# Messages of layer L2 in a four-network graph kernel: half of the tiles' source products built on TensorE and VectorE, the other half gathered

## The reference, cut to what matters

```python
h_src = h[src]
W_rel = jnp.matmul(w_comp, V).reshape(num_rels, in_dim, out_dim)   # 90 x 16 x 16
e = jnp.concatenate([h_src @ Ws.T, he @ Ws.T, h[dst] @ Ws.T], axis=1) @ Wa.T
msg = jnp.einsum('ei,eio->eo', h_src, W_rel[rel_type]) * e
h_out = jax.ops.segment_sum(msg, dst, num_segments=n_nodes)
```

## Time and profile before

| | us |
|---|---|
| median of 3 runs | 8560.5 (8557.9 to 8567.8) |
| the profiled execution, its own time | 8550.3 |
| its span in the profile | 8548.6 |
| the `y_tab` block, in the trace | 5984.4 to 6116.8 |
| `message_pass`, in the trace | 6116.8 to 7202.1 |

### The profile page before, as it was taken

One profiled execution on the slowest core, in us unless ns is written; L12 is line 12 of the kernel. 1 busy time (PEld: TensorE's weight loads), 2 busy tenths in 40 slices (PEclk: granted clock), 3 DMA queues, 4 the chain that ended last, 5 costly groups with the idle time before them and its releaser, 6 DMA issues. The chain is left out here.

```text
span 8548.6 us, 233535 instructions
## 1 busy us (share of the span) xinstructions
PE 6428.4 (75%) x55142; PEld 5292.3 (62%) x55143; DVE 4918.4 (58%) x13561; ACT 2820.3 (33%) x8471; POOL 5192.9 (61%) x7408
## 2 busy tenths in 40 slices
PE   1222215767699998999899989997866666888998
PEld 1111113555477776888688868886455555887998
DVE  7333345867455655666466646664322223998999
ACT  1222212545333333333333333332133333222554
POOL 2777754756477766777577757774277775222554
PEclk8555556555599999999999999998555555999999
DMA  2000003434388886888688878885200001332232
GB/s 66 3 3 3 3 29 104 120 97 120 88 221 216 216 197 181 222 221 222 161 222 222 222 164 223 222 222 121 95 7 7 7 7 24 82 82 57 73 73 59
DMA packets 1319112, 1000.54 MB, mean 117 GB/s; under 512 B 479354, under 2 KB 1223183, under 8 KB 1318092
## 3 DMA queue, kind: packets, MB, share of 16 engines
q1 hardware_dynamic: 941322, 649.30, 27.7%
q0 software_dynamic: 134272, 178.98, 10.8%
q10 hardware_dynamic: 243392, 170.76, 6.9%
HBM read 951.88 MB, written 54.19 MB: 118 GB/s over the span
## 5 line engine op out<-in xcount | busy, mean ns | idle before, releaser
L1480 POOL DMA_INDIRECT qg<-q_tab,qidx x2520 | 2389.2, 948 | 940.1 <-issue 699.2
L1635 DVE COPY ps<-b 128x384 f32<-128x384 f32 x1120 | 628.0, 561 | 1381.2 <-ACT h L1600 1374.8
L1067 PE MATMUL ps<-rhs_i,ohi 128*128 128x128 f32 (+2 forms) x8640 | 1215.7, 266 | 210.1 <-issue 197.2
L1067 PEld LDWEIGHTS ps<-rhs_i,ohi 128*128 128x128 f32 (+1 forms) x8640 | 1000.4, 163 | 342.5 <-issue 282.0
L1033 POOL COPY near<-x 128x48 bf16 x2160 | 675.9, 351 | 789.4 <-PE ps L1056 434.0
L1195 POOL DMA_INDIRECT got_m<-y_tab,idx_m x832 | 815.8, 981 | 478.8 <-issue 251.4
L1549 PE MATMUL ps<-ohm,h 128*128 128x128 f32 x6720 | 1032.9, 290 | 65.3 <-DVE ps L1635 33.9
L1549 PEld LDWEIGHTS ps<-ohm,h 128*128 128x128 f32 x6720 | 838.8, 192 | 257.7 <-issue 242.8
L1593 ACT ACTIVATE h<-ps,b 128x384 f32<-128x384 f32 x1120 | 650.2, 581 | 1052.2 <-PE ps L1531 955.6
L375 POOL DMA_INDIRECT list_by_src<-ring,rpos x808 | 783.1, 969 | 349.0 <-issue 255.0
L1212 PE MATMUL ps<-rhs_m,ohi_m 128*128 x2880 | 668.1, 403 | 416.1 <-ACT rhs_m L1238 387.3
(11 more groups left out here) (442 smaller groups left out, 8623.6 us busy)
## 6 DMA issues: line engine op xcount, KB each, us to landing
pb<-p_tab ACTq DMA_DIRECT2D x1680, 96.0 KB
pb<-p_tab SPq DMA_DIRECT2D x1680, 96.0 KB
places<-place_by_turn SPq DMA_DIRECT2D x560, 192.0 KB
places_i<-place_by_meeting SPq DMA_DIRECT2D x360, 256.0 KB, 3.4
places_i<-place_by_meeting SPq DMA_DIRECT2D x720, 128.0 KB, 3.1
qb<-q_tab SPq DMA_DIRECT2D x840, 64.0 KB
qg<-q_tab,qidx POOLq DMA_INDIRECT x2520
nears<-near_by_turn SPq DMA_DIRECT2D x560, 64.0 KB
```

Of the source, the lines that this page charges most:

```text
L1067: m = pe.matmul(ps[:, bass.ds(to[j], width)], ohi[:, h, j, :], rhs[:, h, j, 0:width], start=False, stop=True, skip_group_check=True)
L1480: pool.indirect_dma_start(qg[:, h, j, :], None, q_tab, IndirectOffsetOnAxis(ap=qidx[:, h, j:j + 1], axis=0)).then_inc(m_got[h], 16)
```

## The change

It splits each group of 4 tiles into the first two and the last two. The last two are gathered from `y_tab` as before. For the first two, the edge's source row (17 numbers: 16 features and the gate's part) comes from a product of a one-hot matrix `ohx` (node place against edge) with the source block's rows `xq`, and the edge's relation matrix (256 numbers) from a product of a one-hot `ohr` (relation against edge) with the 90 matrices in three bf16 parts, `w_parts`. VectorE multiplies the two and sums over the 16 inputs. The sums at the destinations stay as they are, but their place in TensorE's order is now fixed: group N-16 (`LAG` = 16) right behind the products of group N, and the last 168 groups after all products. VectorE's `build` is placed 12 groups behind (`AHEAD = LAG - U`).

More of the change, by code:

```diff
@@ L592, in gnn_kernel @@
             loc_s = sb("loc_s", [P, NT], F32, st)
+            rel_f = sb("rel_f", [P, NT], F32, st)
+            at_x = sb("at_x", [1, NT], I32, st)
+            rel_rows = sb("rel_rows", [P, 8, P], BF16, st)
             blk_s = sb("blk_s", [1, NT], F32, st)
@@ L716, in _ @@
                     v_chain(dve, dve.tensor_scalar(blk_s[0:1, :], blkt[0:1, :], float(P), None, ALU.mult))
+                    v_chain(dve, dve.tensor_scalar(at_x[0:1, :], blkt[0:1, :], 17.0, float((NB - 1) * 17), ALU.mult, ALU.min))
                     dve.wait_ge(b_l, 16)
@@ L836, in _ @@
                     m.then_inc(c_w, 1)
+                    for c in range(8):
+                        m = pe.transpose(banks[6 + c // 4][0:C8, (c % 4) * P:(c % 4 + 1) * P], rel_f[:, c * C8:(c + 1) * C8], ident[:, :])
+                    m.then_inc(c_rel, 1)
                     pe.wait_ge(c_const, 2)
@@ L1164, in summed, with message_pass @@
             return ps[:, 512 * k:512 * k + 56 * n].rearrange("p (b c) -> p b c", c=56)
-        d_idx, d_rhs, d_ohi, d_sum, d_part, d_at = (sem("d_" + n) for n in ("idx", "rhs", "ohi", "sum", "part", "at"))
+        d_idx, d_rhs, d_ohi, d_sum, d_part, d_at, d_oh, d_w, d_xs, d_prod, d_m, d_gate = (
+            sem("d_" + n) for n in ("idx", "rhs", "ohi", "sum", "part", "at", "oh", "w", "xs", "prod", "m", "gate"))
         d_got = [sem(f"d_got{h}") for h in range(U)]
-        def message_pass():
+        d_pl = [sem(f"d_pl{h}") for h in range(U)]
+        LAG = 4 * U
+        assert (LAG - 2) * G >= NT2 - -(-E // P) + NB - 1 and NGI % U == 0 and K > 5
+        def message_pass(xq, w_parts):
             with ExitStack() as st:
-                idx = sb("idx_m", [P, U, G], I32, st)
-                got = sb("got_m", [P, U, G, 17], F32, st)
+                idx = sb("idx_m", [P, U, 2], I32, st)
+                got = sb("got_m", [P, U, 2, 17], F32, st)
                 ohi = sb("ohi_m", [P, U, G, P], F32, st)
@@ L1178, in message_pass, with x_bank @@
                 at_m = sb("at_m", [1, NIN * 2], I32, st)
+                at_x = sb("at_xm", [1, NT], I32, st)
+                pl = sb("pl_m", [P, U, 2 * P], BF16, st)
+                rl = sb("rl_m", [NREL, U, 2 * P], BF16, st)
+                ohx = sb("ohx_m", [P, U, 2 * P], F32, st)
+                ohr = sb("ohr_m", [NREL, U, 2 * P], BF16, st)
+                xs = sb("xs_m", [P, U, 2, 17], F32, st)
+                prod = sb("prod_m", [P, 2, 512], F32, st)
+                def x_bank(h):
+                    return banks[2 + h % 2][:, 0:34].rearrange("p (j f) -> p j f", j=2)
                 with nc.Block() as block:
@@ L1214, in sums @@
                             m.then_inc(d_sum, 1)
-                        turns(pe, sums, KI)
+                        def both(k, h):
+                            products(k, h)
+                            if not isinstance(k, int) or k >= LAG // U:
+                                sums(k * U + h - LAG, h)
+                        for k in range(5):
+                            for h in range(U):
+                                both(k, h)
+                        with pe.Fori(5, K) as k:
+                            for h in range(U):
+                                both(k, h)
+                        with pe.Fori(0, (NGI - NG + LAG) // U) as k:
+                            for h in range(U):
+                                sums(k * U + h + NG - LAG, h)
                     @block.scalar
@@ L1236, in step @@
[L1236 to L1240, removed]
+                            rows(k, h)
+                            if there(k, h, 1):
+                                messages(*moved(k, h, -1))
@@ L1253, in build, with step @@
                                               dst_i[:, bass.ds(n * G, G)][:, :, None].to_broadcast([P, G, P]), ALU.is_equal).then_inc(d_ohi, 1)
-                        turns(dve, build, KI)
+                        AHEAD = LAG - U
+                        def step(k, h):
+                            onehots(k, h)
+                            if there(k, h, 1):
+                                multiply(*moved(k, h, -1))
+                            if not isinstance(k, int) or k * U + h >= AHEAD:
+                                build(k * U + h - AHEAD, h, not isinstance(k, int) or k * U + h >= LAG)
+                            if there(k, h, 1):
+                                add_up(*moved(k, h, -1))
+                        for k in range(5):
+                            for h in range(U):
+                                step(k, h)
+                        with dve.Fori(5, K) as k:
+                            for h in range(U):
+                                step(k, h)
+                        multiply(K - 1, U - 1)
+                        add_up(K - 1, U - 1)
+                        with dve.Fori(0, (NGI - NG + AHEAD) // U) as k:
+                            for h in range(U):
+                                build(k * U + h + NG - AHEAD, h)
         def turn_block(src, f, dst, extra=None):
@@ L1935, in _ @@
                     def _(dve):
+                        split(dve, [w_parts[:, q, :] for q in range(3)], w_rows[:, :], w_left[:, :])
                         v_chain(dve, dve.tensor_copy(wr[:, :, 0:16], wl[:, :, :]))
@@ L1939, in _ @@
                         v_chain(dve, dve.tensor_reduce(s3[:, :], tmp[:, :, :], AX.X, ALU.add))
+                nodes([(xT, a_cols[:, 0:1])], 1, 7)
                 YC = NREL * 17 // 3
```

89 lines of the change are left out of this document (73 added, 16 removed).

## The result

The changed kernel takes **9072.6 us** (median of 4 runs, 9068.5 to 9076.3), the kernel before 8563.9 beside it (4 runs, 8557.9 to 8567.8): ratio 1.0595, 95% interval 1.0581 to 1.0608. It is slower by 509 us. The profiled execution has a span of 9066.8 us, against 8548.6.

The account below looks back on a forecast made before the run. GpSimd's 832 gathers were taken to fill the message stage before the change. With +494 us for the stage and +17 for preparation, the forecast against the median of 8560.5 was 9072 us, range 8970 to 9260.

Parts of the forecast that it names:

- The circle: Message stage, main part: TensorE's step and three VectorE parts alternate without overlap, 6.43 us a step, 192 steps, 1235 us.
- TensorE's part: Products and sums in one main step: 0.86 + 1.28 + 1.75 + 0.16 = 4.05 us.
- To TensorE: Main step, from the end of VectorE's `ohx` to TensorE's products: 0.15 us, between 0.05 and 0.25.
- The first steps: Message stage, steps 0 to 15, without sums: about 3.0 us each, 48 us together.
- The bare sums: End of the message stage: 168 remaining groups of sums with only hidden one-hots beside them, 1.75 us each, 294 us.
- The stage: Whole message stage: 1579 us against 1085.3 before, +494 us.
- The preparation: Work added ahead of the messages, such as `split`, `nodes`, transposes and a load: +17 us, bounds 12 to 25.
- Collisions with GpSimd: Message stage: VectorE and GpSimd hinder each other at shared ports, lengthening the comparisons, up to +92 us more.
- A: Rival: the clock rises in the main part, step 4.5 us, stage 1208 us, 8700 us in all; chance 0.03.
- B: Rival: the clock rises in the last sums as well, -147 us, 8553 us, no change; chance 0.02.
- C: Rival: main part's wait not serial, TensorE runs through, 3.9 us a step, 8585 us; chance 0.05.
- D: Rival: main step of 7.5 us from comparisons kept off by GpSimd and register loads, +205, 9277 us; chance 0.10.

Follow-up runs that it names:

- late `build`: The changed kernel, but in step N VectorE builds the destination one-hots of group N-13 instead of N-12: 8565.2 us, ratio to the kernel before 1.0001.
- short-product run: The changed kernel with two products for the relation matrices a step instead of six, only the first bf16 part used: 8964.6 us, ratio 1.0470.
- quarter version: Built on the changed kernel: one tile of four by products, three gathered, gates by ScalarE, sums spread over the steps: 8358.2 us, ratio 0.9761.
- half: Two tiles of four by products and two gathered, as in the change, but sums spread, seven groups every four steps: 8534.2 us, ratio 0.9971.

## Why the prediction was right

**The circle.** Predicted: a step of 6.43 us, TensorE and three parts of VectorE strictly in turn, by the count N-15 in `build`'s wait. Measured: 6.33 in the mean, and the kernel without that circle (the late `build`) is 507 us faster. Link by link, the steps from the earlier trace rows stand against the means of the trace after (steps 20 to 199, each rounded by itself):

| link | predicted | measured |
|---|---|---|
| TensorE's end to `build` | 0.16 | 0.16 |
| `build` to the reduction's start | 0.60 | 0.61 |
| the reduction to `ohr` | 0.93 | 0.92 |
| `ohr` to `ohx` | 0.19 | 0.19 |
| `ohx` to its end | 0.35 | 0.36 |
| to TensorE | 0.15 | 0.14 to 0.47, mean 0.24 |
| products and sums | 4.05 | 3.86 |
| sum | 6.43 | 6.33 |

Two terms were mis-sized, against each other. **TensorE's part**: the products came as priced (0.87 and 1.23 to the next start, for 0.86 and 1.28), but a group of sums behind products takes 1.75 to its last record's end, not 1.75 and another 0.16. I had taken 0.16 for the last result, from a group that stood alone with 1.91. That longer time belongs to a group whose first weight load starts with its first product, as in the short-product run (1.91 again); behind six products the load starts 0.21 ahead, and the 0.16 falls away. **To TensorE**: the steps repeat as 6.54, 6.36, 6.21, 6.21 us over the four turns of a loop body, and the surplus lies between `ohx` and the first product (0.14 in two steps of four, 0.23 and 0.47 in the others; 0.48 in the timeline above), but for 0.05 of the 6.36, where `ohx` itself takes 0.40. I had bounded the way by 0.05 to 0.25 and missed that two steps of four start later. That it is the jump at the loop's end, and the reading of addresses behind it, is an inference from the period of four; no run took the loop apart.

The reduction, priced by the 1.007 us of L2057, took 0.999: a strided row of the same kind was the right neighbour, and a plain operation of as many elements (0.69) would have made each step 0.3 too short.

**The first steps.** Predicted 3.0 each, 48; measured 40.8 for the sixteen, 2.55 each. A small miss, from GpSimd's addition, which I had bounded by 0.2 to 0.7 and which takes 0.20 in the mean, in part inside the gathers' issue time.

**The bare sums.** Predicted 168 x 1.75 = 294; measured 309 (7411.5 to 7720.9), 1.84 each. A row of them:

```profile
7706.37 7.17 PE L1277 MATMUL ps<-rhs_m,ohi_m 128*128 x32 [0.23 <-issue]
7713.76 7.16 PE L1277 MATMUL ps<-rhs_m,ohi_m 128*128 x32 [0.22 <-issue]
```

Four groups start every 7.39 us: 7.16 of work, 1.79 for one, and 0.23 idle at each turn of the loop. Inside a turn the groups follow each other by 1.75, as priced; what was missing is the turn, 7.39 - 4 x 1.75 = 0.39, 42 times, 16 us. I had the price from six groups in a row with no turn of the loop between them.

**The stage.** 2.7 to the first `ohx`, 40.8, 191 steps in 1208.5 and 4.3 for the last, 309.4: 1565.7, for 1579. The +494 of the prediction measures +481 (against 1084.2).

**The preparation.** Predicted +17 (12 to 25); alone it costs +25 (15 to 34). In the trace after, the messages start 37 us later than before, 14 of it in L2's preparation and 23 ahead of L2, of which the altered code of the sorting part explains up to 7; the rest is spread over code that the change leaves alone. The kernel with the same preparation and the messages of before reached them 6 us sooner (first gather at 6149.5), and the kernel before with only its sums' order changed 9 us later (6126.7) than the kernel before itself (6117.8), with the same code ahead; so a single trace is no good measure of such a sum. The 14 in L2's preparation come again in the trace of the preparation alone, and are what the terms for it had (0.4 + 2.0 + 11.5); the part ahead of L2, put at 3, is the one that was too small. With the interval of the experiment, +25 is the better number, and +481 and +25 make 506 of the 509. That the sum lands on the measured time to 1 us is luck: the 192 steps were put 22 us too long and the first sixteen 7, the bare sums 15 and the preparation 8 too short. The mechanism isn't luck, since each link was named and measured.

**What hid the rest.** GpSimd's gathers fit in: 416 x 0.959 are 399 us of 1566, and in the main part it waits for `xs` (604.7 us in 191 waits). Two figures of the prediction mix busy time and time between gathers. The "some 540" for GpSimd's busy time counted 0.30 between gathers with each; busy it is for 439. And 832 gathers with their issue times take 816 + 251 = 1067, not 1082; the rest of the stage before is its last sums. Neither enters the forecast. The multiplication took 0.68 beside TensorE's products, as supposed.

**Collisions with GpSimd** would have added up to 92. The comparisons in the circle start 0.19 apart, as priced without them, though some last 0.46 instead of 0.28, and the sum grew by no more than the 0.05 of one `ohx` in four. It is the gathers that show them: 1158 against 943 ns as above, and 1021 in the quarter version, where 197 of 624 gathers start inside a `build`. Gathers that start inside the reduction, which reads one operand, are not lengthened: 198 in the change take 949. The Trainium skill, SBUF — State Buffer, "SBUF: two separate sides", has VectorE with two SBUF inputs and a GpSimd operation that reads SBUF keep each other off for a whole instruction. The traces agree in part: `build`, with two SBUF inputs, lengthens a gather and the reduction doesn't, but gathers that start in the first 0.5 us of a `build` take 1219 for 943, so they lose 0.28 in the mean, less than what is left of its 0.69.

**The rivals.** A and B, a rise of the clock: the granted clock is 0.50 in the main part and in the bare sums. With the late `build` TensorE was busy in 700 of 700 us at 0.50, so an unbroken run of these products didn't raise it. C, no circle: the late-`build` kernel is that case, and it came out at 8565 where I had put 8585, with steps of 3.65 for my 3.9. With the measured start, bare sums and preparation, the point from which the change gains lies at (1085 - 2.7 - 40.8 - 309.4 - 25)/192 = 3.68 and not at 3.77; a step of 3.65 is 6 us below it, which is even within the noise. D, longer steps by collisions: none at 7.5; the longest regular one is 6.54.

## What to carry to other kernels

When two engines hand work to each other in both directions, write down for every wait the count it wants and the step in which that count is reached; a wait that is reached in the same step behind the other engine's last work makes a circle, and all that is queued behind it on its engine joins it. One step more of distance costs a buffer slot's lead and no time; here one group of it gave 507 us back. Then ask what the relief of one engine costs the next one: of the two shares tried here a quarter gave 200 us and half 24, and at a quarter the work that had been in the shadow of the gathers was worth 241 us when it was spread over all steps and not left to the end.

## What the runs showed of the hardware

- Being busy all the time doesn't by itself raise TensorE's clock for this mix of products (loads of 128 columns for 17, 32 or 256 columns moved): the granted clock was 0.50 with TensorE busy in 700 of 700 us and in 767.6 of 770. The Trainium skill, TensorE: Matmul & The Clock Gate, Part 1, has sustained activity release the half-rate clock; no run here agrees for these shapes, while L3's pass with 128-column one-hots, at 89% busy, has 1.00.
- A group of eight small products takes 1.75 us behind six products with 256 columns, where its first weight load starts 0.21 ahead, and 1.91 behind two, where load and product start together. The way from the first of them to the group is 0.60 for two and 1.23 for six: taking four products away gave back 0.50 of the expected 0.85.
- The same gather takes 951, 959, 981 and 1021 ns in the mean in four versions. It isn't VectorE's share that counts: 959 belongs to the change, where VectorE is busy for 42%, and 981 to the kernel before with 23%. It is what VectorE is doing when the gather starts. In the kernel before, 111 gathers start in the first 0.5 us of a `build` and take 1219, all others 943 to 950. In the change the fixed places in a step keep them apart: only 2 of 416 start there, while 198 start inside the reduction, at 949. In the run with the copy in the reduction's place some 190 gathers start inside the one-hot comparisons (L1349 and L1350) and take 1152 and 1088, and the mean is 1016.
